# Routing a mixture of experts in three batches, two of them inside the edge stream of a graph layer

## What is computed

```python
x = x + gnn(layernorm(x), edge_attr_64, node_vec1, src, dst, W_self, W_func, W_att)
x = x + ffn(layernorm(x)[None], router_w, w1, w2, w3)[0]

def gnn(h, w, snorm_n, edge_src, edge_dst, ...):
    z = h @ W_func.T
    e = leaky_relu(concat([z[edge_src], z[edge_dst], w]) @ W_att.T)
    alpha = softmax of e over the edges of one destination
    agg = segment_sum(alpha * z[edge_src], edge_dst)
    return h + relu(where(has_edge, h @ W_self.T + agg, h))

def ffn(x, ...):
    probs = softmax(x @ router_w.T)                 # 8 experts
    top 2 probs, divided by their sum + 1e-9, are the gates
    y_e = (silu(x @ w1[e].T) * (x @ w3[e].T)) @ w2[e].T
    return sum over e of gates[e] * y_e
```

## Time and profile before

| | us |
|---|---|
| median of 3 runs | 1058.5 (1057.94 to 1058.61) |
| profiled execution, span | 1057.7 |
| TensorE busy in the span | 833.1 (79%) |
| VectorE busy | 619.6 (59%) |
| ScalarE busy | 450.1 (43%) |
| GpSimd busy | 575.1 (54%) |

### The profile page before, as it was taken

One profiled execution on the slowest core, in us unless ns is written; L12 is line 12 of the kernel. 1 busy time (PEld: TensorE's weight loads), 2 busy tenths in 40 slices (PEclk: granted clock), 3 DMA queues, 4 the chain that ended last, 5 costly groups with the idle time before them and its releaser, 6 DMA issues.

```text
span 1057.7 us, 18646 instructions
## 1 busy us (share of the span) xinstructions
PE 833.1 (79%) x4388; PEld 695.9 (66%) x4389; DVE 619.6 (59%) x2073; ACT 450.1 (43%) x1063; POOL 575.1 (54%) x556
## 2 busy tenths in 40 slices
PE   7955879865865775775777921899999999999995
PEld 6812444644654664664565711899999999999995
DVE  6524555555665666666656668456566565656553
ACT  4323243464565456456456730234344343443331
POOL 1177777777777777777775000635353544434332
PEclk9986998987887888788788955899999999999998
DMA  7775666565554545555454250452534522222221
GB/s 241 209 250 187 189 199 183 143 180 173 149 141 133 148 133 141 141 142 143 133 158 116 68 190 1 124 114 48 115 67 89 116 44 46 35 41 40 40 41 20
DMA packets 81139, 128.83 MB, mean 122 GB/s; under 512 B 21356, under 2 KB 56689, under 8 KB 80577
## 3 DMA queue, kind: packets, MB, share of 16 engines
q0 software_dynamic: 30720, 69.90, 28.6%
q1 hardware_dynamic: 43145, 51.59, 15.7%
q10 hardware_dynamic: 7200, 6.56, 1.8%
HBM read 106.86 MB, written 17.86 MB: 118 GB/s over the span
## 4 chain that ended last, share of the span: by engine, by line
PE 54%; DMA 11%; issue 11%; POOL 10%; DVE 9%; DVEq 2%; POOLq 0%; ACT 0%; SPq 0%; ACTq 0%
PE bank L1311 17%; PE bank L1237 13%; POOL early L780 8%; DMA early<-ztab,early 8%; PE bank L1350 6%; PE bank L1201 3%; PE bank L1340 3%; PE bank L1357 2%; PE bank L1083 2%; PE bank L1168 2%; PE bank L1165 2%; PE bank L1099 1%; DMA out_rows<-late,slot_rows 1%; DVE acc L1607 1%; POOL out_rows L824 1%
## 5 line engine op out<-in xcount | busy, mean ns | idle before, releaser
L780 POOL DMA_INDIRECT early<-ztab,early x416 | 396.4, 953 | 173.2 <-issue 170.5
L1311 PE MATMUL bank<-split_w,operands 128*128 x1344 | 237.7, 326 | 2.8 <-DVE operands L1839 1.4
L1237 PE MATMUL bank<-early,W 128*128 128x258 f32 x832 | 232.4, 432 | 6.5 <-DVE W L1584 6.0
L1311 PEld LDWEIGHTS bank<-split_w,operands 128*128 128x128 f32 x1344 | 213.6, 190 | 9.4 <-issue 7.4
L1237 PEld LDWEIGHTS bank<-early,W 128*128 128x128 f32 x832 | 172.0, 216 | 55.0 <-issue 23.6
L831 POOL DMA_INDIRECT xg<-ttab,slot_rows x56 | 57.6, 1028 | 230.4 <-DVE late L1866 180.2
L982 ACT ACTIVATE W<-early 128x128 f32<-128x128 f32 x208 | 91.0, 484 | 128.1 <-PE bank L1237 124.7
L1201 PE MATMUL bank<-ident,early 128*16 128x128 f32 x104 | 24.2, 380 | 138.7 <-DVE early L1567 138.7
L1201 PEld LDWEIGHTS bank<-ident,early 128*16 128x16 f32 x104 | 10.3, 120 | 150.6 <-DVE early L1567 148.0
L824 POOL DMA_INDIRECT out_rows<-late,slot_rows x56 | 88.9, 1588 | 34.0 <-issue 15.6
L1052 ACT ACTIVATE late<-bank 128x384 f32<-128x384 f32 x56 | 27.5, 491 | 187.6 <-PE bank L1311 187.6
(11 more groups left out here) (232 smaller groups left out, 1320.8 us busy)
## 6 DMA issues: line engine op xcount, KB each, us to landing
W<-in_wt SPq DMA_DIRECT2D x26, 512.0 KB, 4.8
W<-in_experts SPq DMA_DIRECT2D x40, 266.5 KB, 2.8
early<-ztab,early POOLq DMA_INDIRECT x416, 2.8
W<-in_experts SPq DMA_DIRECT2D x3, 2132.0 KB, 11.7
early<-in_x SPq DMA_DIRECT2D x26, 128.0 KB, 2.2
early<-ztab SPq DMA_DIRECT2D x25, 128.0 KB
early<-late SPq DMA_DIRECT2D x25, 128.0 KB
out_rows<-early ACTq DMA_DIRECT2D x25, 128.0 KB, 1.9
```

The source lines that it names most:

```text
L780: nc.gpsimd.indirect_dma_start(out=zg[:, k * KG + c, :], out_offset=None, in_=ztab, in_offset=bass.IndirectOffsetOnAxis(ap=src_here[:, k / ...
L1237: last = mm(ps[2 + k // 2 % 2][:, 0:ZR], prob_hot[:, k % 3, c * P:(c + 1) * P], zg[:, k * KG + c, :], start=(k % 2 == 0 and c == 0), stop= ...
L1311: last = mm(bank[:, 0:n], x[:, (k % 2 * KC + c) * P:(k % 2 * KC + c + 1) * P], split_w[:, bass.ds(at + (part + w + c * H), n)], start=(i = ...
```

## The change

**Layout and branch.** The general way stands first in the code, the common way in the `Else`; GpSimd waits for the table inside its way. **Node tiles.** Tile 24 runs one step behind tile 23 (`LAST_AT`) and uses bank 0 for transpose and logits. **Routing.** It is done for tiles 0 to 8, 8 to 16 and 16 to 25. The first two batches are a stage of lag 34 in the stream, on VectorE, ScalarE (the exponential) and TensorE: batch 0 in steps 62 to 77, batch 1 in steps 94 to 109. One batch is a first choice, a second choice, a prefix sum along the tiles, gates, three matmuls for ranks (with what earlier batches counted, `seen`), and for each choice of each tile two one-hots, `hot_row` (256 columns) and `hot_cell` (100 columns, times the token's number), both in fp16, in chunks of three, a ring of two chunks; TensorE adds their products up in bank 1 as a table of 256-row cells. Behind the last batch two matmuls pick cells into slots. The softmax's quotient is taken for the gates alone. **Fillers.** `stay_busy` issues matmuls with no reader: two in each of the steps 119 to 127, 20 behind the last batch's ranks, three behind each chunk, 10 and 30 around the last two matmuls, eight behind the first row transpose. **Expert weights.** ScalarE makes the high parts of expert 0 and 1 behind the last exponential; VectorE's low part of expert 0 is two pieces, one behind the expert list, one behind the first tile's transpose; the first `up` waits for the first piece only, the first `down` for the second. SyncE loads expert 1 when the last sums are added and stores the gates in two parts, with the load of expert 2 behind. When an expert is split is now named by three tables (`split_both`, `split_act`, `slot_done`), which VectorE fills in the first two turns.

```diff
+BUSY_FROM, BUSY_TO = GROUPS - SETTLED - 7, GROUPS - SETTLED + 2
+LAST_AT = BATCH * (TILES - 2) + 1
+ROUTES = ((0, 8), (8, 16), (16, TILES))
+ROUTE_RING = 2
+CHUNK = 3
...
+        def early_route(t):
+            for b, (lo, hi) in enumerate(ROUTES[:-1]):
+                i = t - BATCH * (hi - 1)
+                if 0 <= i < 9 + CHUNKS_OF[b]:
+                    return b, i
+            return None, None
...
-            with eng.If(bad_at == 0):
+            with eng.If(bad_at > 0):
+                general()
+            with eng.Else():
                 in_order()
-            with eng.Else():
-                general()
...
             def at_group(t, k, r):
+                if t == LAST_AT:
+                    stage(TILES - 1, (TILES - 1) % NODE_RING, (TILES - 1) // NODE_RING)
                 j = r * NODE_RING + k // BATCH
-                if k % BATCH or (isinstance(j, int) and j >= TILES):
+                if k % BATCH or j >= TILES - 1:
                     return
                 stage(j, k // BATCH, r)
...
+                sp.wait_ge(sums_added, GROUPS // 2)
+                sp.wait_ge(next_added, GROUPS // 2)
+                expert_load(1)
+                gates_store()
+                expert_load(2)
...
-            pool.wait_ge(z_stored, 16 * len(BLOCKS))
             def in_order():
+                pool.wait_ge(z_stored, 16 * len(BLOCKS))
...
+                exp_of(len(ROUTES) - 1)
+                act.wait_ge(experts_in[0], 16)
+                act.wait_ge(sums_psum, GROUPS)
+                split_hi(act, 0)
+                second_hi()
+                keep_tokens()
...
+            def stay_busy(n):
+                for _ in range(n):
+                    mm(ps[3][:, 0:2 * P], iota_h[:, 0:P], iota_h, start=True, stop=True)
+            def route_rest(first):
+                for b in range(first, len(ROUTES)):
+                    rank_of(b)
+                    stay_busy(20)
+                    for i in range(CHUNKS_OF[b]):
+                        tokens_of(b, i)
+                        stay_busy(3)
+                stay_busy(10)
+                slots_of()
+                stay_busy(30)
+            def tokens_of(b, i):
+                pe.wait_ge(onehot_ready, chunk_no(b, i) + 1)
+                for q, j, at in chunk(b, i):
+                    last = mm(ps[1][0:HALF_CELLS, 0:2 * P], hot_cell[:, at, :], hot_row[:, at, :], start=(b == 0 and q == 0), ...)
+                last.then_inc(token_psum, 1)
...
+                    b, i = early_route(t)            # TensorE, lag 34
+                    if BUSY_FROM <= t < BUSY_TO:
+                        stay_busy(2)
+                    if i == 6:
+                        pe.wait_ge(top_ready, min(ROUTES[b][1] + 8, GROUPS // BATCH))
+                        rank_of(b)
+                    elif b is not None and i >= 9:
+                        tokens_of(b, i - 9)
...
+            def one_hots(b, i):
+                if chunk_no(b, i) >= ROUTE_RING:
+                    dve.wait_ge(token_psum, chunk_no(b, i) - ROUTE_RING + 1)
+                for q, j, at in chunk(b, i):
+                    v.tensor_scalar(hot_row[:, at, :], iota_h, row_of[:, q:q + 1], None, ALU.is_equal)
+                    last = v.tensor_scalar(hot_cell[:, at, :], iota_h[:, 0:HALF_CELLS], cell_f[:, q:q + 1], token_id[:, j:j + 1],
+                                           ALU.is_equal, ALU.mult)
+                last.then_inc(onehot_ready, 1)
...
+                def route(t, k, r):                  # VectorE, lag 34
+                    b, i = early_route(t)
+                    if i == 0: first_choice(b)
+                    elif i == 1: second_choice(b)
+                    elif i == 2: prefix_of(b)
+                    elif i == 3: gates_of(b)
+                    elif i == 7: ranks_of(b)
+                    elif b is not None and 8 <= i < 8 + CHUNKS_OF[b]: one_hots(b, i - 8)
...
-                for piece in range(2):
-                    pe.wait_ge(lo_split[piece], e + 1)
+                pe.wait_ge(lo_split[0], e + 1)
                 if at_least(t, 1):
+                    pe.wait_ge(lo_split[1], e + 1)
                     pe.wait_ge(hid_a_ready, t)
```

More of the change, by code:

```diff
@@ L153, in carve @@
                 n *= d
-            words = n if dt != bf16 else n // 2
+            words = n if dt != fp16 else n // 2
             v = region[:, at:at + words]
@@ L188, in build @@
         src_in, o = carve(ef, o, [LOADS, KG], i32)
+        hot_cell, o = carve(ef, o, [ROUTE_RING * CHUNK, HALF_CELLS], fp16)
+        iota_h, o = carve(ef, o, [2 * P], fp16)
+        gates, o = carve(ef, o, [TILES, E])
+        same, o = carve(ef, o, [E, RB])
         assert o <= 5 * WE
@@ L731, in _ @@
             sp.sem_inc(finish_over, 1)
-            sp.wait_ge(gates_ready, 1)
-            sp.dma_start(ttab[:, C:TR].rearrange("(t p) e -> p t e", p=P), gates).then_inc(gates_stored, 16)
-            sp.wait_ge(gates_stored, 16)
+            for e in range(RAW):
+                sp.wait_ge(experts_in[e], 16)
+                sp.sem_inc(raw_in, 1)
             for e in range(RAW, E):
@@ new lines, in _, with route @@
+            links_before = count[0]
+            def in_order():
+                count[0] = links_before
+                def route(t, k, r):
+                    b, i = early_route(t)
+                    if i == 0:
+                        first_choice(b)
+                    elif i == 1:
+                        second_choice(b)
+                    elif i == 2:
+                        prefix_of(b)
+                    elif i == 3:
+                        gates_of(b)
+                    elif i == 7:
+                        ranks_of(b)
+                    elif b is not None and 8 <= i < 8 + CHUNKS_OF[b]:
+                        one_hots(b, i - 8)
@@ L1812, in _ @@
[L1812 to L1821 removed]
+            split_lo(dve, v, 0, 0)
```

535 lines of the change are left out of this document (324 added, 211 removed).

## The result

The changed kernel takes 1052.46 us (1051.76 to 1053.91, four runs) against 1058.55 (1057.94 to 1058.91, four runs): a ratio of 0.9942, 95% interval 0.9929 to 0.9956. It is faster, by 0.6%, but 17.9 us slower than the 1034.6 that I had forecast, and outside the range of 1026 to 1043.

A forecast was written before the change was run, and what follows sets the result against it. GpSimd's gathers bound the stream, TensorE the drain and expert stage, VectorE's routing the stretch between. Last logits 615.4 + routing 18.7 + 7.85 put the first expert matmul at 641.95, 23.9 us earlier: 1058.5 - 23.9 = 1034.6 us, range 1026 to 1043.

The forecast's parts named there:

- In the loops, the turns in which an expert is split come out the same: Expert stage: splitting the next expert's weights in the loop costs no more than before; 0 in the sum, without a bound.
- T0: Time when the last logits are there: forecast 615.4 us (bounds 612.5 to 619) from four terms, against 614.96 before.
- term 1: Stream start: GpSimd branches before waiting for the z table, so the stream starts 0.9 us earlier (bounds 0 and 1.8).
- term 2: Engines jump at the start, where waits hide it, instead of the end; the 2.74 us gap behind the last logits goes.
- term 3: Batches 0 and 1 routed inside the stream: 0.6 us for slower gathers, 2.5 us for batch 1 in the drain.
- rival A: VectorE's one-hot operations lock GpSimd's gathers out through the shared port: 6.4 instead of 0.6 us lost, 1040.4 us; chance 0.08.
- B: VectorE's idle time in the stream cannot be used and the sums slip: 10.8 us lost, 1045.4 us; chance 0.06.
- C: No slack: VectorE becomes the stream's bound, both early batches (28.8 us) lie on the path, 1063.4 us; chance 0.03.
- Term 4: Last node tiles: tile 24 one step behind tile 23, interleaved with fillers, gains 1.8 us (bounds 0.5 and 3).
- Slot table to U0: Way from the slot table to the first expert matmul (U0, forecast 641.95): kept at 7.85 us (bounds 5.8 and 8.4).
- First tiles: First expert tiles: a higher clock's gain against later splits, tables and gathers; taken as 0 (bounds -1.9 and +1.5).
- D: Fillers fail: the clock stays at 1.2 GHz through routing and tile 0; +1.8 us, 1036.4 us; chance 0.08.

The follow-up runs named there:

- the four edits: Changed kernel with VectorE's low piece ahead of `gated`, no second table read on ScalarE, expert 1's load behind last logits, GpSimd's common way behind its branch: 1036.77 us.
- the five edits: The four edits on the changed kernel, plus tile 24 back four steps behind tile 23: 1033.5 us, and 1033.62 us when repeated in five rounds.

## Why the prediction was wrong

**The step that failed most** is "In the loops, the turns in which an expert is split come out the same": 11.8 us of the 17.9. I had costed the split's instructions, which are indeed the same, and not their place. The diff moves VectorE's piece from ahead of `gated` to behind it. There a 3.1 us operation stands in VectorE's queue ahead of the next turn's first multiply and of the low part of the hidden tile behind that, for which TensorE's down matmuls wait; ahead of `gated` it delays an output for which TensorE shows no wait. That alone is 10.1 us of the stage in the profile, 8.0 in the medians. ScalarE's second table read, which I did not price at all, is 3.9 us with the piece behind `gated` and 1.3 with it ahead. The view that would have warned me was at hand: the earlier trace rows has TensorE at 99.28 of 100 us, so whatever delays the two engines that feed it past their slack is on the path. These loops stood at 0 in the sum without a bound: even with all other terms at the late ends of their own bounds, 13.5 us, it comes to 1048.1, short of the 1052.46 measured.

**T0** came 6.6 us late: the last gather 2.0 (573.73, where terms 1 and 3 make 571.7), the way from there to the last sums 0.3 early (2.2 us longer than before, where 2.5 was forecast), the way from the last sums to the last logits 4.9 late (3.1 longer, where 1.8 less was forecast). The bounds of 612.5 to 619 were narrower than those of the terms, which add up, with the 1 us for a late store, to 610.7 to 622.5; the 621.98 measured lies in the latter.

**T0, term 1** (the branch ahead of the wait, -0.9): wrong in sign for the changed kernel. The mechanism that I named is there, and the run with the old order on GpSimd shows it whole, a first gather at 46.69. But term 2 went through VectorE, TensorE, ScalarE and SyncE and asked of each whether a jump at the start is hidden, and left out GpSimd, the one engine on which the start hangs. Its jump took 7.6 us. The Trainium skill (Runtime: NRT & Kernel Launch, Instruction fetch mechanics) says that a taken branch out of the fetched window stalls until its target is fetched by DMA. The gap and the transfer of the kind "instruction" in it (48.86) agree, and so does the 2.74 us gap of before, which has such a transfer at 615.82. Why this jump took so long isn't shown. The DMA engines were busy for 92 to 100% of 44 to 50 us, but VectorE and TensorE jumped in 4.5 and 5.2 us at 56% (57.0 to 61.8), and the 2.74 us before fell in a stretch at 70% (614.96 to 617.70).

**Terms 2 and 3**: term 3 held, and term 2 held for the other engines. The 2.74 us behind the last logits are gone. VectorE's jump at the start of the changed kernel shows as "issue", and a wait for a gather stands behind it, so it is hidden, as I had said; TensorE's 5.2 us have a wait of 3.9 us for weights behind them:

```profile
62.08 0.17 DVE L1837 TENSOR_TENSOR early<-edge_sb,early 128x4 f32<-128x4 f32 x1 [4.45 <-issue]
...
71.31 0.17 DVE L1837 TENSOR_TENSOR early<-edge_sb,early 128x4 f32<-128x4 f32 x1 [5.33 <-DMA early<-ztab,early]
```

No gather waited longer for TensorE, and the gathers' mean is unchanged, so neither rival A (the port), nor B, nor C came about, and the 0.6 us for the port were not needed. For A the mean of all gathers says little, as only eleven of the 416 lie beside a one-hot operation; these eleven average 0.96 us, the longest 1.01. The 1.15 us that I put down to VectorE were a misreading: the gather of 48.67 was over before the operation of 50.43 began. In the run with the old order on GpSimd the first gather (46.69) takes 1.15 us while VectorE is idle until 48.72, and one beside two such operations (49.43) takes 0.94. The drain's price for batch 1, 2.5 us, measured 2.6.

**Term 4** (tile 24, -1.8): wrong in sign. I counted the gap between two tiles as waiting time that interleaving would fill, and did not look at what TensorE's queue then holds: a transposition that waits for ScalarE, in front of the tile that was ready. The pull costs 1.0 to 2.6 us with the load there and 1.6 to 3.1 without it, part of it at the lower clock level, at which the last router matmuls of the run with the four edits are. The way from the last sums to T0 grew from 14.0 to 17.1 us; without load and pull it was 13.5, so these two made at least 3.6, and the rest gained 0.5.

**SyncE's load** ("nothing in the sum waits for these stores before the rows are gathered, cost 0, and 1 us if one is late"): 2.0 us or more. The stores' data are not waited for, but their buffers are: `residual` of a later tile writes into them.

**The routing**, 18.7: measured 19.1, and 18.9 to 19.3 in the runs that route two batches early. The prices by number of elements carried over.

**Slot table to U0**, kept at 7.85: 5.24. I moved the low piece by 1.5 us in my working and kept the gather's 3.03 us, which came from that very piece. The bound of 5.8 that I gave for a gather of 1 us was the better number.

**First tiles**, 0: with the misplaced work put back and the second table read gone the stage takes 392.8 us against 391.9, inside the bounds that I gave for these tiles. **D** (no effect of the fillers on the clock) did not come about: the first `up` took 2.36 us, not 4.20.

That the five edits together land at 1033.6, near the 1034.6 forecast, is no success of the sum but luck: that run reached U0 = 637.58 and not 641.95, by terms that erred in both directions, and it is five edits away from the kernel of the forecast.

## What to carry to other kernels

When a diff moves an instruction within a turn of a loop that keeps another engine full, price what stands behind it in its queue, not the instruction. When a program is laid out anew around a branch, go through all engines, and first the one that works first. Before two chains are interleaved on an engine with a fixed order, ask which of their waits will now stand in front of work that is ready, and for a load that is drawn forward, which buffers are freed by the transfers beside it.

## What the runs showed of the hardware

- A gather or scatter that GpSimd starts while VectorE subtracts two operands in SBUF (3.11 us) does not end until that is done: 3.03 us (635.28 and 658.86), 3.23 (643.09) or, for the scatter, 3.98 us (709.81), against 0.95 and 1.59 alone. The gathers end 0.82 or 0.83 us after VectorE's operation, the six scatters of the changed kernel 1.46. The Trainium skill (SBUF — State Buffer, SBUF: two separate sides) says that of a VectorE operation with two inputs in SBUF and a GpSimd operation that reads SBUF, the one that starts first gets the shared port for the whole instruction and the other is blocked. These rows agree for the GpSimd side: gather and scatter read their row numbers from SBUF (`slot_rows`) and are held when VectorE was first. The other side isn't seen: the piece of 709.20 began 0.3 us before a gather was over (708.52 to 709.50) and took the same 3.12 us as alone. The eleven gathers of the stream beside one of the routing's one-hot operations (0.2 to 0.3 us) averaged 0.96 us.
- A jump across the code of the general way showed no work for 7.6 us on GpSimd, 5.2 on TensorE and 4.5 on VectorE at the start of the changed kernel, and for 2.74 on VectorE at the end of the stream before.
- A 2.1 MB weight load doubled the landing time of 128 KB stores beside it, from 1.8 to 3.9 us.
